# A transformer block pair on one Trainium2 core: one sum tensor for the first expert loop, and four folds ahead of the second attention

## What is computed

```python
x = x + tanh(g_xattn[0]) * L0_xattn(layernorm(x), ctx, ctx, ...)      # sigmoid attention on 64 context tokens
x = x + tanh(g_ffn[0])   * L0_ffn(layernorm(x), gate_w, W1, b1, W2, b2, sW1, sb1, sW2, sb2)
x = x + tanh(g_xattn[1]) * L1_xattn(ctx, layernorm(x), Wq, bq, Wk, bk, Wv, bv, gamma, beta)
x = x + tanh(g_ffn[1])   * L1_ffn(layernorm(x), Wr, W1, b1, W2, b2)
```

## Time and profile before

| | |
|---|---|
| device time, 3 runs | 700.84 us median (700.63 to 704.89) |
| profiled execution | 704.9 us, its span 702.2 us, mean granted clock 0.992 |
| busy in the span | PE 667.3 us (95%), weight load 569.3 (81%), DVE 450.3 (64%), ACT 450.8 (64%), POOL 296.2 (42%) |
| chain that ended last | PE 75%, DVE 7%, DMA 7%, ACT 3%, issue 3%, POOL 2% |

### The profile page before, as it was taken

The page is one execution under the profiler, slowest core; times in us unless marked ns, Lnnn a source line. Parts: engine busy times, 40 slices in busy tenths (PEclk is TensorE's granted clock), DMA queues, the critical chain, the costliest instruction groups (busy, mean ns, idle before and its releaser), DMA issues.

```text
span 702.2 us, 21726 instructions
## 1 busy us (share of the span) xinstructions
PE 667.3 (95%) x7504; PEld 569.3 (81%) x7505; DVE 450.3 (64%) x1150; ACT 450.8 (64%) x1150; POOL 296.2 (42%) x221
## 2 busy tenths in 40 slices
PE   6999999999899999999999989998999999999992
PEld 4533766689799899898999979766999999999992
DVE  4867664758788675666745479985986545544541
ACT  3564776555399777776765548934997566566561
POOL 1102443445626565554555332402454545455432
PEclk9999999999999999999999999999999999999997
DMA  8983021236189766999866389954544444444432
GB/s 277 370 281 93 1 31 54 69 93 240 53 264 245 141 136 141 241 200 249 220 140 120 57 246 418 370 208 125 135 77 75 79 79 77 81 68 76 77 50 22
DMA packets 110678, 104.96 MB, mean 149 GB/s; under 512 B 53067, under 2 KB 96085, under 8 KB 109734
## 3 DMA queue, kind: packets, MB, share of 16 engines
q1 hardware_dynamic: 95126, 83.27, 39.6%
q0 software_dynamic: 14976, 20.58, 18.4%
q10 hardware_dynamic: 528, 0.52, 0.2%
HBM read 64.84 MB, written 28.23 MB: 133 GB/s over the span
## 4 chain that ended last, share of the span: by engine, by line
PE 75%; DVE 7%; DMA 7%; ACT 3%; issue 3%; POOL 2%; SPq 1%; POOLq 0%; DVEq 0%; ACTq 0%
PE bank L1279 9%; PE bank L1277 9%; PE bank L1278 9%; PE bank L1290 9%; PE bank L1292 9%; PE bank L1291 9%; PE bank L1402 2%; PE bank L1016 2%; PE bank L964 2%; DMA x_arena<-token_rows,gather_now 2%; PE bank L1018 1%; PE bank L1017 1%; PE bank L1165 1%; PE bank L1167 1%; PE bank L1166 1%
## 5 line engine op out<-in xcount | busy, mean ns | idle before, releaser
L1629 ACT ACTIVATE work<-bank,b_cols 128x128 f32<-128x128 f32 x624 | 176.0, 385 | 134.7 <-PE bank L1279 130.2
L1277 PE MATMUL bank<-x_arena,weights 128*128 128x128 f16 x1248 | 213.1, 219 | 3.2 <-DMA x_arena<-x_arena 1.8
L1278 PE MATMUL bank<-x_arena,weights 128*128 128x128 f16 x1248 | 213.1, 219 | 0.1
L1279 PE MATMUL bank<-x_arena,weights 128*128 128x128 f16 x1248 | 213.1, 219 | 0.0
L2121 DVE TENSOR_TENSOR work<-work 128x512 f16<-128x512 f32 x156 | 101.0, 689 | 126.5 <-ACT work L1637 113.7
L1290 PE MATMUL bank<-weights,work 128*128 x624 | 170.2, 273 | 1.9 <-issue 1.2
L1292 PE MATMUL bank<-weights,work 128*128 x624 | 170.1, 273 | 0.0
L1291 PE MATMUL bank<-weights,work 128*128 x624 | 170.1, 273 | 0.0
L847 POOL DMA_INDIRECT x_arena<-token_rows,gather_now x78 | 82.8, 1061 | 139.2 <-DVE gather_now L2115 96.2
L1277 PEld LDWEIGHTS bank<-x_arena,weights 128*128 x1248 | 122.1, 98 | 5.6 <-issue 3.2
L1278 PEld LDWEIGHTS bank<-x_arena,weights 128*128 x1248 | 122.1, 98 | 0.8
(11 more groups left out here) (247 smaller groups left out, 1160.6 us busy)
## 6 DMA issues: line engine op xcount, KB each, us to landing
weights<-in_L_ffn_W SPq DMA_DIRECT2D x76, 256.0 KB, 7.3
raw<-in_L_ffn_W SPq DMA_DIRECT2D x44, 256.0 KB
split_dram<-row_arena SPq DMA_DIRECT2D x12, 512.0 KB
weights<-split_dram SPq DMA_DIRECT2D x3, 2048.0 KB, 16.9
odd_sum<-padding_row SPq DMA_DIRECT2D x1, 2176.0 KB, 12.6
token_rows<-row_arena SPq DMA_DIRECT2D x1, 2072.0 KB, 7.0
weights<-in_L_ffn_sW SPq DMA_DIRECT2D x8, 256.0 KB, 7.2
x_sum<-x_arena SPq DMA_DIRECT2D x4, 512.0 KB, 4.7
```

Of the source, the lines that this page charges most:

```text
L1277: nc.tensor.matmul(o, w1_at[f][c][0].block(), hi, start=c == 0, stop=False)
L1278: nc.tensor.matmul(o, w1_at[f][c][0].block(), lo, start=False, stop=False)
L1279: m = nc.tensor.matmul(o, w1_at[f][c][1].block(), hi, start=False, stop=c == DC - 1)
L1629: m = nc.scalar.activation(hid[:, k, f * P:f * P + P], h_ps[k][half][:, g * P:g * P + P], ACT.Gelu, bias=b1_cols[n][:, f, bass.ds(e, 1)], ...
```

## The change

1. `odd_sum`, its filling with zeros, its loads and the four `merge` steps go. All tiles of the first loop add to `x_sum[0]`; each add waits for the one before it, and POOL's order (gather, then add) stays.
2. Each batch's `kv` products and each batch's fold get a PSUM bank of their own. The masks run batch by batch behind the products. All four folds come ahead of `turned1(0, ...)`; the banks of the attended output are swapped, so that batch 0's lies where batches 0 and 1 were folded.
3. The centring of Wq moves from `second_keys` into the first loop's end, ahead of the last tile's `result`, with a semaphore for its load.
4. ACT does `folded_out(2)` ahead of `deviations(0)`; `turned1` and `x_statistics` wait for the load itself.

```diff
-            sp.dma_start(odd_sum.rearrange(...), padding_row...broadcast_to([P, TT + 1, D])).then_inc(padded, 16)
-            sp.wait_ge(padded, 48)
+            sp.wait_ge(padded, 32)
...
             sp.wait_ge(down_done[0], ROUTED)
-            sp.wait_ge(added_odd, 16 * (ROUTED // 2))
+            sp.wait_ge(added[0], 16 * ROUTED)
             for b in range(B):
-                if b == 0:
-                    sp.dma_start(odd_rows[b], batch_of(odd_sum, b)).then_inc(in_x[b], 16)
-                    sp.wait_ge(added[0], 16 * (ROUTED + 1) // 2)
                 sp.dma_start(x_sb[:, TB * b:TB * b + TB, :], batch_of(x_sum[0], b)).then_inc(in_x[b], 16)
-                if b:
-                    sp.dma_start(odd_rows[b], batch_of(odd_sum, b)).then_inc(in_x[b], 16)
...
                 def add(j, q, k):
-                    sums, done = (odd_sum, added_odd) if n == 0 and k else (x_sum[n], added[n])
-                    if n == 0 and at_least(j, 2):
-                        pool.wait_ge(done, 16 * q)
-                    elif n and at_least(j, 1):
-                        pool.wait_ge(done, 16 * j)
+                    if at_least(j, 1):
+                        pool.wait_ge(added[n], 16 * j)
                     pool.wait_ge(y_ready[n], j + 1)
                     pool.sem_inc(turn_taken, 1)
                     nc.gpsimd.indirect_dma_start(
-                        out=sums, ...).then_inc(done, 16)
+                        out=x_sum[n], ...).then_inc(added[n], 16)
...
-            pe.wait_ge(dve_setup, 8)
             folded(0)
             pe.wait_ge(act_setup, 5)
             pe.wait_ge(y_read[0], ROUTED)
             folded_bias(0)
-            pe.wait_ge(dve_setup, 9)
+            folded(2)
...
             def turned1(b, h):
-                pe.wait_ge(ln_done, 2 * B + 2 * b + 2)
+                pe.wait_ge(in_x[b], 32)
...
                 for h in range(2):
                     attention1(b, h)
                 if b == 0:
-                    folded(2)
                     folded_bias(2)
...
             folded_bias_out(0)
+            folded_out(2)
             deviations(0)
-            folded_out(2)
             folded_out(3)
...
                     dve.wait_ge(down_done[n], j + 1)
-                    if n and at_least(j, 2):
+                    if at_least(j, 2):
                         dve.wait_ge(added[n], 16 * (j - 1))
-                    elif at_least(j, 2):
-                        dve.wait_ge(added_odd if k else added[0], 16 * q)
...
                 splitting_loop(dve, n, body)
+                if n == 0:
+                    centred_queries()
                 result(ROUTED - 1, (ROUTED - 1) // 2, (ROUTED - 1) % 2)
...
-            merge(0)
             x_statistics(0)
-            merge(1)
             x_statistics(1)
-            merge(2)
             add_beta(0)
             x_statistics(2)
-            merge(3)
```

More of the change, by code:

```diff
@@ L255, in build @@
         kv_ps = bank[6:8]
-        key_ps, pair_ps = bank[0:2], bank[2:4]
-        fold_ps = bank[4:6]
+        key_ps, pair_ps = bank[0:2], bank[2:4] + bank[0:2]
+        fold_ps = bank[4:6] + bank[2:4]
         def scores_ps(n):
@@ L869, in add @@
                     nc.gpsimd.indirect_dma_start(
-                        out=sums, out_offset=bass.IndirectOffsetOnAxis(ap=add_now[:, k:k + 1], axis=0),
-                        in_=y_sb[:, k, :], in_offset=None, compute_op=ALU.add).then_inc(done, 16)
+                        out=x_sum[n], out_offset=bass.IndirectOffsetOnAxis(ap=add_now[:, k:k + 1], axis=0),
+                        in_=y_sb[:, k, :], in_offset=None, compute_op=ALU.add).then_inc(added[n], 16)
                 def body(j, q, k):
@@ L1354, in _ @@
                 for c in range(DC):
-                    m = nc.tensor.matmul(pair_ps[b % 2][:, (b // 2 * DC + c) * P:(b // 2 * DC + c) * P + P], kv1[r, 0, b // 2, c * P:c * P + P],
+                    m = nc.tensor.matmul(pair_ps[b][:, c * P:c * P + P], kv1[r, 0, b // 2, c * P:c * P + P],
                                          kv1[r, 1, b // 2, c * P:c * P + P], start=True, stop=True)
-            m.then_inc(pe_setup, 1)
+                m.then_inc(pairs_done, 1)
             def folded(first):
-                for i in range(2):
-                    if first:
-                        pe.wait_ge(act_setup, 6 + i)
+                for b in range(first, first + 2):
+                    pe.wait_ge(pairs_masked, B if first else b + 1)
                     for c in range(DC):
@@ L1365, in folded @@
                             at = c * D + e * P
-                            m = nc.tensor.matmul(fold_ps[i][:, at:at + P], late_wq[:, e, c * P:c * P + P], kv_block[:, first + i, e, :], start=True, stop=e != c)
+                            m = nc.tensor.matmul(fold_ps[b][:, at:at + P], late_wq[:, e, c * P:c * P + P], kv_block[:, b, e, :], start=True, stop=e != c)
                             if e == c:
-                                m = nc.tensor.matmul(fold_ps[i][:, at:at + P], ident, ident, start=False, stop=True)
+                                m = nc.tensor.matmul(fold_ps[b][:, at:at + P], ident, ident, start=False, stop=True)
                     m.then_inc(pe_setup, 1)
@@ L1655, in folded_out @@
                 for c in range(DC):
-                    m = nc.scalar.activation(kvm[:, b, c, :], fold_ps[b % 2][:, c * D:c * D + D], ACT.Identity, bias=kvm_mean[:, b, c:c + 1])
+                    m = nc.scalar.activation(kvm[:, b, c, :], fold_ps[b][:, c * D:c * D + D], ACT.Identity, bias=kvm_mean[:, b, c:c + 1])
                 m.then_inc(act_setup, 1)
             def folded_bias_out(first):
-                act.wait_ge(pe_setup, 12 + first // 2 * 3)
+                act.wait_ge(pe_setup, 11 + first // 2 * 3)
                 for b in range(first, first + 2):
@@ L2232, in shift1 @@
                 V.scalar_tensor_tensor(mid_shift[:, i, :], mid_mv[:, i, :, 0], -1.0, mid_rstd[:, i, :], ALU.mult, ALU.mult).then_inc(shift_ready, 1)
-            def merge(b):
-                dve.wait_ge(in_x[b], 48)
-                V.tensor_tensor(batch(b), batch(b), odd_rows[b], ALU.add).then_inc(ln_done, 2)
             def x_statistics(b):
-                dve.wait_ge(ln_done, 2 * B + 2 * b + 2)
+                dve.wait_ge(in_x[b], 32)
                 statistics1(lambda t: x_sb[:, TB * b + t, :], 0)
```

44 lines of the change are left out of this document (21 added, 23 removed).

## The result

| | before | after |
|---|---|---|
| median of 20 runs, us | 700.93 (698.47 to 708.74) | 707.21 (704.02 to 712.87) |
| ratio of the two, 95% interval | | 1.0086 [1.0069, 1.0104], by it +6.0 us |
| profiled execution / span, us | 704.9 / 702.2 | 706.73 / 704.0 |
| mean granted clock of the profiled execution | 0.992 | 0.991 |

The kernel is slower by 0.9%. In the changed kernel the add is L859 (L869 before), the gather L840, DVE's copy of the row numbers L2119 (L2133), the folds L1355/L1357 (L1366/L1368), the bias product L1364 (L1375), the turn of x L1379 (L1391), the attention product L1390 (L1402).

What follows compares the result with a forecast made beforehand. PE sets the quiet pace and the second attention; adds end last in crowds. Against profiled 704.9 us, x's load 9.2 later, merge −1.4 and folds −2.68 give +5.1: 710.0, or 706.0 on the median; range 698.5 to 716.

Steps and rivals of the forecast that it cites:

- Part 1: Between the loops: folds ahead of x's first turn take 2.68 us off PE's chain, costing at most 0.8 before it.
- Part 2: Between the loops: without batch 0's merge, PE turns x about 0.1 us after its load instead of 1.49, −1.4 us.
- Part 3: At the start: SP no longer waits 12.1 us for zero filling; taken as 0, between −0.5 and 0.
- Part 4a: First loop's add chain: POOL needs about 0.9 us from one add's landing to the next add.
- Part 4b: Crowded stretch from 212 us: serial adds delay the next gather and its transposes; PE loses +1.5 us, bounds 0 and +5.
- Part 4c: Crowded stretch 281 to 347 us: 12 tiles, chain loses 9.6 us, slack takes 5.6, PE loses 4.0; bounds 0 and +20.
- Part 4d: First loop's end: 1.5 us of the chain's lag is left, and tile 38's add waits for tile 37's, +2.2 us.
- The rival that PE cools: Ahead of x's first turn: idle PE drops to its lower clock, 2 to 4 us more, 708 to 710; chance 0.08.
- The rival that the adds hide: First loop: lone adds take 4 to 5 us even in crowds, so PE loses nothing there; 698.5 to 702, chance 0.30.
- The full crowded price: Second crowded stretch: spreading tiles does not relieve the adds, +18 instead of +4.0, 719 to 720; chance 0.12.

Runs made afterwards that it cites:

- folds_only: The kernel before with only the folds, masks and centring changed, both sum tensors and merges kept; 703.33 us against 701.58, ratio 1.0001.
- the five serial profiles: Profiles at normal traffic of the changed kernel and four variants whose first-loop adds each wait for the one ahead; medians 702.55 to 710.39 us.
- the light one: Kernel before and changed kernel, both with the staging traffic taken away; 700.83 and 700.00 us, ratios 0.9962 and 0.9941.
- folds_only_again: Second timing of the kernel before with only folds, masks and centring changed; 699.66 us against 701.80, ratio 0.9977.
- one_sum_only: The kernel before with a single sum tensor and serial adds, no zeros, second loads or merges, folds as they were; 709.37 us, ratio 1.0094.
- the heavy pair: Kernel before and changed kernel, both with 256 KB more written to DRAM behind each stage; 706.19 and 709.05 us, ratios 1.0040 and 1.0080.
- before_keep: The kernel before with six filling matmuls in the router's two PE gaps; 699.98 us against 701.80, ratio 0.9962.
- two_sums_serial: The kernel before, both tensors and merges kept, with each first-loop add also waiting for the previous tile's add; 710.39 us, ratio 1.0114.
- keep_clock: The changed kernel with 12 filling matmuls on PE during its wait for x; 706.89 us, ratio 1.0060 to the kernel before.

## Why the prediction was right, and where its sizes were not

The forecast of 706.0, slower by less than 1%, held: 707.21, ratio 1.0086. The mechanism was right: the adds wait for each other, fall behind the tiles in the crowd, and x's first load hangs on the last of them. That the figure came out within 1.2 us is partly luck, as the steps show:

- **Part 1, folds, −2.68 behind the turn and at most 0.8 before it: right.** folds_only has −2.70 and +0.79. In the changed kernel they lie under the wait for x, as forecast. Products and folds started later than the 409.3 that I took (411.43), for the loop itself ended 2.1 us later.
- **Part 2, merge, −1.4: right.** PE turns 0.04 us behind the load's end (420.21 to 420.25) instead of 1.49.
- **Part 3, zeros, 0: right.** The first add goes at 206.1 to 207.4 us in the profiles that have them and at 205.4 to 207.2 in those that don't.
- **Part 4a, wake 0.9: right.** 0.79 and 0.80 at the end, 0.82 to 0.89 in the crowd (chain).
- **Part 4b, first crowd: too dear for the adds.** I let serial adds take the 7.4 to 9.1 us of the overlapping ones. They took 6.73, 5.75 and 6.12, and tile 2's went at 219.85, not 221.0; the gather at 221.96, not 223.8.
- **Part 4c, second crowd: right in kind, the term mis-sized.** Add 5.4 and tile 6.3 us were forecast, 9.6 us lost by the chain and 4.0 by PE. Measured: a tile every 5.91 us, so an add of 5.05 when the wake of 0.86 is taken off, 5.2 us lost by the adds from tile 14 to 26 (2.9 to 7.2 over the five serial profiles). PE's loss of 4b and 4c together, 5.5 us in the forecast, shows at the keys as 2.1; as 3.0, if counted from the first add, which was 0.9 earlier in this profile. Over five profiles of each kind it is 1.3 on average, with overlapping ranges: PE's share was far too dear, and may be nothing.
- **Part 4d, the end: +2.2 for the last add right, the 1.5 left from the crowd too cheap.** The last two adds are 4.58 apart where I had 4.7. But tile 37's add was 4.9 us late and the keys 2.1, which leaves 2.8 in place of 1.5; from the keys to the last add it was 4.9 us more than before where I had 3.7, and 5.3 to 7.3 more in the other four serial profiles. Together the last add is 7.0 us late, not 9.2 (7.5 on average of five against five); x is turned at 420.25, not 422.7. Of the 5.5 us for 4b and 4c, 3.4 were too dear, and 1.3 of that came back here.
- **The rival that PE cools** was given 0.08 and did occur in this profile, at 1.5 us. I had priced it as an addition to a rare case. Of the 14 profiles 13 have such a drop between 400 and 480 us, the kernel before too (0.50 at 455.9 to 459.3), at changing places. So they belong to both sides of the comparison. By the marks the turn's 5.35 us less the folds' 2.68 give +2.7, and only the drop makes that +4.2 at the router's first turn. The two errors, adds too dear and clock left out, partly cancelled: +5.1 forecast, +6.0 measured.
- **The rival that the adds hide** was wrong for this traffic and right for the light one, where the loop's end moves by 0.4 us. Its premise, that the long adds are long through each other, is partly borne out: the adds of tiles 1, 2 and 3 take 6.8 to 7.4, 7.3 to 8.0 and 7.0 to 9.2 us where they overlap (DVE's releases less the issue, in before, folds_only and folds_only_again), and 6.4 to 7.5, 5.2 to 5.8 and 4.4 to 6.1 in the five profiles of serial adds at normal traffic. It decides at 4.9 us, and the serial adds of the second crowd stayed at 5.05 in the changed kernel's profile, 4.85 to 5.2 over the five: normal traffic lies close to the border.
- **The full crowded price** (8.3 us a tile) was excluded by the same 12 tiles, 5.7 to 6.1 us each in the five serial profiles.

The rule of the Trainium skill that was weighed there, the page "DMA: Bandwidth & Descriptors", section on the anatomy of one DMA on GpSimd's path, would give an estimate of 2.3 us for such an add. The traces disagree. In the chains of these runs no add of the first loop took under 3.47 us; quiet ones took mostly 3.7 to 4.0, crowded ones 5 on average and up to 7.45 (one_sum_only, tile 1).

Open: of the +6.0 us the profiled executions themselves show only 1.8 (706.73 against 704.9), because the one of before had a drop in the router and the changed one's came earlier and cost 1.5. The marks up to the router's start give +4.2 (443.30 to 447.52); the remaining 1 to 2 us of the medians are within what drops add or take away, and no run settles them. Open too is why the heavy pair's times lie closer together than the normal pair's.

## What to carry to other kernels

A chain of accumulating DMAs that wait for each other had here a pace of landing plus some 0.8 us; compare it with the tile's time in the stretch where DMA traffic is highest, not where it is quiet, since there the slack is gone. Count the lag that the chain brings to the loop's end, and its last links, at full price, for everything behind the loop hangs on the last landing. In these profiles that lag was the surer part of the loss, and PE's delay in the loop the smaller one. If a gain of 2 us in the profile does not show in the median, look at the mean granted clock of all runs on both sides, and measure again. Half a change may be better than the whole: the folds alone with filled gaps beat both kernels.

## What the runs showed that I had not expected

Granted clock and time go together over the runs of one kernel: the correlation is −0.73 for the 20 of the changed kernel, and −0.79, −0.77, −0.61 and −0.53 for the 23, 24, 29 and 17 of the one before in four sessions. So some 30 to 60% of the variance goes with the lower level's share, not all of it. One such spell of 3.4 us costs some 1.5 us (the attention product's 5.21 against 3.69), and gaps of 0.42 and 0.85 us stood ahead of the one in the router; six products into them were worth 1.8 us between the medians in one session (before_keep 699.98, before 701.80; by the ratio 0.38%, 2.7 us), though a spell came all the same, later.

The first loop itself differs between profiles of kernels that are the same there: the keys come at 403.58 (before), 405.88 and 400.31 (folds_only twice). Marks of single profiles carry some 3 us of that, and a difference as the +2.1 at the keys means nothing by itself: in one session the serial one_sum_only, two_sums_serial and keep_clock had their keys at 404.3 to 404.7, ahead of the 405.88 of folds_only with its free adds.
